# Attention and routed FFN on one core: inputs laid out by the host, attention weights expanded by VectorE and ScalarE in turn, softmax normalised earlier

## The reference, cut to what matters

```python
# x, ctx: (32, 128, 256) float32, 4096 tokens in 32 tiles of 128
# per token: 16 heads of 16 channels attend to each other inside the token
q = layernorm(x) @ Wq.T + bq ; k = ctx @ Wk.T + bk ; v = ctx @ Wv.T + bv
logits = einsum('bsid,bsjd->bsij', q, k) / 4        # 16 x 16 for every token
out = einsum('bsij,bsjd->bsid', softmax(logits), v)
x = x + transpose(out, (0, 2, 1, 3)).reshape(b, s, 256) @ Wd.T + bd
h = layernorm(x); gates = softmax((h @ w_red) @ normalised(wg).T)   # 8 experts
e = argmax(gates)                                    # one expert per token
x = x + (gelu(h @ W1[e] + b1[e]) @ W2[e] + b2[e]) * max(gates)
```

## Time and profile before

| | |
|---|---|
| median of 3 runs | 432.7 us |
| profiled execution | 430.04 us, span 428.1 us |
| PE, DVE, ACT, POOL busy | 89%, 73%, 55%, 69% of the span |
| granted TensorE clock, mean | 0.979 of full speed |
| DMA | 59.31 MB, 97433 packets |

### The profile page before, as it was taken

The page is one execution under the profiler, slowest core; times in us unless marked ns, Lnnn a source line. Parts: engine busy times, 40 slices in busy tenths (PEclk is TensorE's granted clock), DMA queues, the critical chain, the costliest instruction groups (busy, mean ns, idle before and its releaser), DMA issues.

```text
span 428.1 us, 11390 instructions
## 1 busy us (share of the span) xinstructions
PE 381.1 (89%) x3791; PEld 303.4 (71%) x3791; DVE 310.9 (73%) x667; ACT 234.8 (55%) x783; POOL 297.2 (69%) x399
## 2 busy tenths in 40 slices
PE   6996999999999989998888687978999999999980
PEld 6774676676766657565555466767999999999970
DVE  3746899899998989999999665579456555555640
ACT  4443778787686877776752564571344444444420
POOL 2767678787687877776775964656387777787751
PEclk9999999999999999999999899999899999999996
DMA  7696866978779787886566501131022222222200
GB/s 163 207 264 164 228 173 209 268 193 239 184 211 260 190 229 181 230 209 175 133 155 185 154 27 39 52 116 48 29 64 75 64 75 74 61 69 65 65 17 0
DMA packets 97433, 59.31 MB, mean 139 GB/s; under 512 B 70366, under 2 KB 88447, under 8 KB 97376
## 3 DMA queue, kind: packets, MB, share of 16 engines
q1 hardware_dynamic: 92368, 48.44, 41.8%
q0 software_dynamic: 3744, 9.53, 7.8%
q10 hardware_dynamic: 1264, 0.61, 0.8%
HBM read 37.41 MB, written 22.07 MB: 139 GB/s over the span
## 4 chain that ended last, share of the span: by engine, by line
PE 34%; DMA 24%; DVE 14%; issue 9%; SPq 9%; POOL 7%; ACT 2%; DVEq 1%; ACTq 0%; POOLq 0%
DMA qkv_scr<-qkv 21%; PE bQ L1107 14%; PE bKV L1075 8%; PE bL L1075 7%; SPq L248 4%; POOL kx L374 3%; SPq L252 2%; SPq L283 2%; DMA b2b<-in_L_ffn_wg 2%; DVE qkv L485 2%; PE bT L1089 2%; DVE qkv L492 1%; DMA ql<-qkv_scr 1%; PE bO L1057 1%; POOL r L420 1%
## 5 line engine op out<-in xcount | busy, mean ns | idle before, releaser
L374 POOL TENSOR_TENSOR kx<-ql,mask 128x2048 f32<-128x2048 f32 x32 | 117.6, 3675 | 42.7 <-issue 32.9
L1107 PE MATMUL bQ<-w,wA 128*128 x312 | 74.3, 381 | 3.4 <-DVE r L721 2.8
L475 DVE TENSOR_TENSOR ax<-bA,mask 128x2048 f32<-128x2048 f32 x32 | 73.3, 2290 | 0.6 <-PE bA L1013 0.6
L1107 PEld LDWEIGHTS bQ<-w,wA 128*128 128x128 f32 x312 | 56.2, 190 | 10.6 <-issue 4.5
L924 PE MATMUL bKV<-wA,xcT 128*128 128x512 f32 x128 | 60.2, 593 | 0.0
L397 POOL DMA_INDIRECT out<-r,isc x39 | 41.3, 1059 | 22.3 <-issue 13.4
L420 POOL DMA_INDIRECT r<-row_scr,ig x39 | 40.5, 1038 | 6.0 <-issue 2.4
L862 ACT ACTIVATE wA<-bL,r 128x128 f32<-128x128 f32 x76 | 21.6, 367 | 41.3 <-PE bL L1075 26.7
L862 ACT ACTIVATE wA<-bKV,r 128x128 f32<-128x128 f32 x80 | 22.8, 367 | 36.1 <-issue 18.8
L355 POOL TENSOR_TENSOR rs<-ve,half 128x2 f32<-128x2 f32 x39 | 28.3, 726 | 20.3 <-ACT ve L742 20.2
L932 PE MATMUL bL<-kx,pad 128*32 128x128 f32 x1024 | 35.8, 282 | 6.8 <-POOL kx L374 6.8
(11 more groups left out here) (202 smaller groups left out, 724.5 us busy)
## 6 DMA issues: line engine op xcount, KB each, us to landing
qkv_scr<-qkv SPq DMA_DIRECT2D x32, 384.0 KB, 4.2
ql<-qkv_scr SPq DMA_DIRECT2D x32, 384.0 KB, 4.6
row_scr<-cat SPq DMA_DIRECT2D x32, 133.5 KB, 3.6
w1b<-in_L_ffn_W SPq DMA_DIRECT2D x16, 256.0 KB, 4.5
w<-in_L_ffn_W SPq DMA_DIRECT2D x16, 256.0 KB, 4.7
xt<-in_x SPq DMA_DIRECT2D x15, 256.0 KB, 4.9
ct<-in_ctx SPq DMA_DIRECT2D x15, 256.0 KB, 4.9
b2b<-in_L_ffn_b SPq DMA_DIRECT2D x4, 256.0 KB, 4.7
```

The costliest lines, as they stand in the source:

```text
L374: eng.tensor_tensor(block(kx[:, z % 2, :]), spread_heads(ql[z % 2][:, :, 0:HD]), mask_b, ALU.mult).then_inc(S["kx"], 1)
L475: eng.tensor_tensor(block(ax[:, :]), spread_heads(bA[:, 0:C].rearrange("p (l i) -> p l i", l=NH)), mask_b, ALU.mult).then_inc(S["ax"], 1)
L1107: i_ = eng.matmul(bQ[:, 0:C], hT[b % 2][:, k, :], w2[:, bass.ds(eb * (KH * C) + k * C, C)], start=(k == 0), stop=(k == KH - 1))
```

## The change

The host passes other layouts of the same numbers: `xc` holds x and ctx turned (per pair of tiles, 4 KB in a row for each partition), `x` is given once more by rows, the weights `wkvT`, `wqT`, `wdT` are turned already, W1 and b1 come as one array and W2 with each partition's data in a row. The turning on TensorE and the copies to `xcT` go. The centring of Wq is made by a matmul with a constant matrix. x is thus read twice.

A ninth gate column (`NL = NE + 1`, each of its weights -1/256) gives minus the row mean out of the matmuls, so that `moments` of the new row needs no pass for the mean. The scaling by 1/256 and the epsilon move from ScalarE to GpSimd, whose two results go straight to `cat`.

`expand` on VectorE writes blocks 4 to 7 only; ScalarE writes blocks 0 to 3 in four instructions (`scalar_expand`) after it and behind `pad` and the row's scaling. This holds for the 28 tiles with `s1 + 4 < 32`; the last four stay on VectorE. Summing and scaling of the softmax (`normed`) stands behind the maximum and the expansion instead of at the end of the iteration; TensorE turns `a2` ahead of Wd. `fill` issues 16 in setup and 3 in each of iterations 0 to 3.

```diff
-EXT = C + NE
+NL = NE + 1
+EXT = C + NL
-CT = 6
+XC = 4
+SHARE = 4
...
         def sync_setup(eng):
-            for w, src in ((1, Wk), (2, Wv), (0, Wq)):
-                eng.dma_start(wst[w], src.rearrange("(a p) c -> p a c", p=P)).then_inc(S[f"ld_w{w}"], 16)
-            for k, src in enumerate((bk, bv, bq)):
-                eng.dma_start(bqkv[:, k, :], src.rearrange("(o n) -> o n", o=1).broadcast_to((P, C))
-                              ).then_inc(S["ld_b"], 16)
+            eng.dma_start(wT[:, :, 0:2 * C], wkvT).then_inc(S["ld_wkv"], 16)
+            eng.dma_start(wT[:, :, 2 * C:3 * C], wqT).then_inc(S["ld_wq"], 16)
+            eng.dma_start(bqkv[:, :, :].rearrange("p k c -> p (k c)"), bkvq.broadcast_to((P, 3 * C))
+                          ).then_inc(S["ld_b"], 16)
...
                 if live(n) and n % 2 == 0:
-                    eng.dma_start(xt[:, n % XR:n % XR + 2, 0:C], x[n:n + 2].rearrange("n p c -> p n c")
-                    eng.dma_start(ct[:, n % CT:n % CT + 2, :], ctx_in[n:n + 2].rearrange("n p c -> p n c")
+                    eng.dma_start(xt[:, n % XR:n % XR + 2, 0:C], x[n // 2]).then_inc(S[f"ld_x{n // 2 % 3}"], 16)
+                c = t + 3 if t > 0 else t + 5 if t == -3 else NT
+                if live(c) and c % 2 == 0:
+                    if c >= XC:
+                        eng.wait_ge(S["qq"], c - XC + 2)
+                    eng.dma_start(xcT[:, c % XC:c % XC + 2, :, :], xc[c // 2]).then_inc(S[f"ld_c{c // 2 % 2}"], 16)
...
+        def normed(eng, s0):
+            eng.wait_ge(S["exp"], s0 + 1)
+            eng.tensor_reduce(sm[:, :], pr.rearrange("p (g j) -> p g j", g=NH), AX, ALU.add).then_inc(S["sm"], 1)
...
...
+                if live(s1) and live(a):
+                    expand(eng, s1)
+                if live(s0) and live(a):
+                    normed(eng, s0)
                 if live(w):
                     eng.wait_ge(S["wd"], w + 1)
...
-                if live(s1) and live(a):
-                    expand(eng, s1)
                 if live(a) and t >= 4:
                     vector_kv(eng, a)
...
+        def scalar_expand(eng, s1):
+            eng.wait_ge(S["ax0"], s1 + 1)
+            for b in range(SHARE):
+                i_ = eng.activation(block(ax[:, :])[:, :, b, :], bA[:, 0:C].rearrange("p (l i) -> p l i", l=NH), ACT.Copy,
+                                    scale=mask[:, b:b + 1])
+            i_.then_inc(S["ax"], 1)
...
         def tensor_setup(eng):
             eng.wait_ge(S["ident"], 1)
-            fill(eng, 12)
-            weight_transposes(eng, 1)
-            tensor_turned(eng, 0)
-            fill(eng, 4)
-            weight_transposes(eng, 2)
-            fill(eng, 6)
-            weight_transposes(eng, 0)
+            fill(eng, 16)
...
                 if t < 4:
-                    fill(eng, 10, bA)
+                    fill(eng, 3, bA)
```

More of the change, by code:

```diff
@@ L73, in slotted, with build @@
     return 0 <= s < NS
-def build(nc, x, ctx_in, Wq, bq, Wk, bk, Wv, bv, Wd, bd, w_red, wg, W1, b1, W2, b2, out):
+def build(nc, x, xc, wkvT, wqT, wdT, Wd, bkvq, bd, bd_col, w_redT, wgT_in, wg, W1b, W2, b2, out):
     f32, bf16, i32 = mybir.dt.float32, mybir.dt.bfloat16, mybir.dt.int32
@@ L156, in build @@
         x0, x1 = fl(kx), fl(pad)
-        wst = [x0[:, 2048 + 512 * w:2560 + 512 * w].rearrange("p (a c) -> p a c", a=KC) for w in range(4)]
-        wrp, wrT = (b2b[:, k * C:(k + 1) * C].rearrange("p (a c) -> p a c", a=KC) for k in range(2))
+        wst = x0[:, 2048:2560].rearrange("p (a c) -> p a c", a=KC)
+        wrT = b2b[0:NG, 0:C]
+        mean = b2b[:, C:C + P]
         wrc = b2b[:, 4 * C:5 * C].rearrange("p (a c) -> p a c", a=KC)
@@ L298, in pool_setup @@
             eng.memset(ident[:, :], 0.0).then_inc(S["filled"], 1)
+            eng.memset(mean, -1.0 / C)
+            eng.memset(gate[:, :, NE:NL], -1.0 / C)
             eng.memset(half[:, :], -0.5)
@@ L480, in vector_kv @@
             if a == 0:
[L481 removed]
+                eng.wait_ge(S["ld_b"], 16)
             if a > 1:
@@ L1155, in _, with laid_out, blocks @@
                     tensor_inverse(eng)
-_INS = ["x", "ctx_1024", "L0_xattn_Wq", "L0_xattn_bq", "L0_xattn_Wk", "L0_xattn_bk", "L0_xattn_Wv",
-        "L0_xattn_bv", "L0_xattn_Wd", "L0_xattn_bd", "L0_ffn_w_red", "L0_ffn_wg", "L0_ffn_W1",
-        "L0_ffn_b1", "L0_ffn_W2", "L0_ffn_b2"]
+def laid_out(inputs, np):
+    def blocks(w, n):
+        return w.reshape(n, P, -1).transpose(1, 0, 2)
+    i = {k.replace("L0_xattn_", "").replace("L0_ffn_", ""): np.asarray(v) for k, v in inputs.items()}
+    x, ctx = i["x"], i["ctx_1024"]
+    xc = np.stack((x.reshape(NT, P, KC, P), ctx.reshape(NT, P, KC, P)), 2).transpose(0, 4, 2, 3, 1)
+    return {
+        "x": x.reshape(NT // 2, 2, P, C).transpose(0, 2, 1, 3),
+        "xc": xc.reshape(NT // 2, 2, P, 4, P).transpose(0, 2, 1, 3, 4),
+        "wkvT": np.concatenate((blocks(i["Wk"].T, KC), blocks(i["Wv"].T, KC)), 2),
+        "wqT": blocks(i["Wq"].T, KC),
+        "wdT": blocks(i["Wd"].T, KC),
+        "Wd": i["Wd"],
+        "bkvq": np.concatenate((i["bk"], i["bv"], i["bq"])).reshape(1, 3 * C),
+        "bd": i["bd"],
+        "bd_col": np.broadcast_to(i["bd"].reshape(KC, P).T[:, :, None], (P, KC, P)),
+        "w_redT": i["w_red"].T,
+        "wgT": i["wg"].T,
+        "wg": i["wg"],
+        "W1b": np.concatenate((i["W1"].reshape(NE, KC, P, HID).transpose(0, 2, 1, 3).reshape(NE, P, KC * HID),
+                               i["b1"].reshape(NE, KH, P).transpose(0, 2, 1)), 2),
+        "W2": i["W2"].reshape(NE, KH, P, C).transpose(0, 2, 1, 3).reshape(NE, P, KH * C),
+        "b2": i["b2"],
+    }
 def kernel(**inputs):
```

318 lines of the change are left out of this document (118 added, 200 removed).

## The result

The changed kernel is slower: 433.97 us (median of 20 runs) against 429.97 for the one before (20 runs). The ratio is 1.0072, with a 95% interval of 1.004 to 1.0104. All ratios in this document compare fast runs alone; here these have means of 433.17 and 430.08 us, and three slower runs of the changed kernel and one of 1331 us of the kernel before are left out. The forecast was 6.5 us faster, 426.2, with a range up to 433; measured is 3.1 us slower, so the sign was wrong too. (The 432.7 that the prediction started from was the median of three runs, and the 2.66 us that it added for the median's distance from the profiled execution are not there over 20 runs: 429.97 against 430.04.)

The account below looks back on a forecast made before the run. It took SyncE's store-and-load loop and a nearly equal three-iteration loop to bound tiles 4 to 23, VectorE the next tiles. Terms -3.8 + 2.0 - 4.2 - 0.5 = -6.5 us gave 426.2 us, range 417 to 433 (eight in ten).

Parts of the forecast that it names:

- What bounds the kernel: Tiles 4 to 23: SyncE's loop of 6.64 us without compute engines, beside a three-iteration loop of 6.66 us per iteration.
- the price of the loads in steady attention: Tiles 4 to 23: 256 KB more for two tiles cost 0.25 us, 0.12 per tile, bounds 0 and 0.25.
- The term for tiles 4 to 23: Steady attention: mean interval from 6.685 to 6.79 us, +2.0 us in all, ends -2 and +6.
- The prediction's own sign of being wrong: A first store after 15 us, steady intervals under 6.5 or over 7.1, or four expansions taking over 2 us.
- the ring-order sentence: Each DMA engine consumes descriptors in ring order; so loads issued behind a store cannot delay it, price nothing in SyncE's loop.
- The loads rival: Tiles 4 to 23: x read twice makes ql land later every second iteration, period 7.0, total 431.4 us; chance 0.17.
- The way through the engines: Three-iteration loop: 0.25 us added from ql to the maximum, 0.15 from the maximum to qad; 20.0 becomes 20.5.
- The slow rival: ScalarE's expansion waits behind pad and holds bO, bL and the maximum: period 7.23, total 438.8 us; chance 0.11.
- The engines rival: Engines were the true limit; freed, they let all intervals fall to about 6.45 us, total 417.4; chance 0.17.
- Tiles 23 to 31: VectorE, the bound, loses 1.1 us; interval falls from 7.58 to 7.05, -4.2 us, VectorE busy below 6.3.
- Setup: Start: wg issued sooner lands near 7 us, first store near 12 instead of 15.84, -3.8 us, range -5 to -1.
- Rest: Last tiles and first slots: ScalarE has 0.9 us less a tile, -0.5 us, range -2 to +1.5.

Follow-up runs that it names:

- loads_behind: Changed kernel with the loads of x and xc issued behind the load back of ql instead of ahead of it; ratio 1.0445 to the kernel before.
- expert_ahead: spread_xc with the half expert issued ahead of SyncE's wait for its store instead of behind the load back; ratio 0.9687 to the kernel before.
- after_no_x: Changed kernel without the loads of x by rows from tile 12 on, so its numbers are other ones; ratio 0.9802 to the kernel before.
- before_extra: Kernel before with one more 256 KB load of x, read by nobody, in each odd iteration from the third on; ratio 1.011 to the kernel before.
- before_ahead: Kernel before with only the half expert's issue moved ahead of SyncE's wait for its store; ratio 0.9862 to the kernel before.
- spread_share_off: spread_xc with the whole expansion on VectorE for all tiles and none on ScalarE; ratio 0.9975 to the kernel before.
- spread_norm_late: spread_xc with sum, inverse and scaling of the softmax back at the end of VectorE's iteration; ratio 0.9972 to the kernel before.
- odd_two: Changed kernel with the 512 KB load of xc as two DMAs of 256 KB in the same odd iteration; ratio 1.0151 to the kernel before.
- after_ahead: Changed kernel with only the half expert's issue moved ahead of SyncE's wait for its store; ratio 0.9773 to the kernel before.
- spread_both: spread_xc with x by rows also loaded one tile (128 KB) in every iteration; ratio 0.9898 to the kernel before.
- spread_xc: Changed kernel with xc loaded one tile (256 KB) in every iteration instead of two tiles in every second one; ratio 0.9876 to the kernel before.
- spread_wg_first: spread_xc with the gate's three small loads first on ScalarE's queue, ahead of xc and x of tile 0; ratio 0.992 to the kernel before.
- spread_setup: spread_xc with tile 0's xc first on SyncE's queue, the gate's loads first on ScalarE's, and 28 unused transposes instead of 16; ratio 0.9933 to the kernel before.

## Why the prediction was wrong

**What bounds the kernel.** Right: SyncE's loop of store, load back and expert, with no engine in it. The half expert's 1.25 us was taken for a cost of issuing. Most of it was a wait behind `ql`, as loads_behind and expert_ahead show (0.4 to 0.6 us once it stands elsewhere, but for a few of 1.1 to 1.3).

**The step that failed** is the price of the loads in steady attention: "512 KB cost about 0.5 us in a pair, and 256 KB more in larger pieces 0.25, or 0.12 per tile". It measured 0.81 us a pair (after against after_no_x), which is 0.40 per tile and above the upper end of 0.25; in the kernel before it was 0.45 a pair (before_extra). The term for tiles 4 to 23, +2.0 us with the ends -2 and +6, was +8.8, outside its own bounds. Of that 7.0 us came from tile 7 on, where after_no_x takes all of it back. The other 1.8 came in tiles 4 to 6 (21.3 us against 19.4), where after_no_x is no faster (21.9); no run takes that part apart. The fault was the linear step from one price to the next. Most of the idle fifth of the DMA engines lay in the even iterations (share 0.68, against 0.91 in odd ones), while the added bytes went into the odd ones. The share of a stretch says nothing on its halves. The prediction's own sign of being wrong, steady intervals over 7.1, came true.

Beside it stood the ring-order sentence from the Trainium skill (DMA: Bandwidth & Descriptors, "Queues, rings and completion order"). The conclusion that I drew from it, that loads behind the store cannot delay it, did not hold: the wait for the store grew from 4.70 to 5.17 in odd iterations, and fell to 4.21 in loads_behind. More of the loss, 0.76 us, came from the issue behind `ql`. What the rule says of order fits loads_behind, where the wait of the next store grew to 6.13 us with more ahead of it.

**The loads rival** named the mechanism and gave 431.4 with a period of 7.0. The period measured 7.15, and its price too was too small: it still had the whole 1.3 us faster, where 3.1 us slower was measured.

**The way through the engines.** I added 0.25 us from `ql` to the maximum and 0.15 from the maximum to `qad`. Neither came. On the mean of tiles 6 to 19 the first way (from `kx`) went from 4.97 to 4.88 us, the second from 5.32 to 5.17. The rows of tile 20 answer to the earlier trace rows and show why `kx` still covers ScalarE (GpSimd, ScalarE, TensorE; start us, us):

```profile
164.82 3.67 POOL L360 TENSOR_TENSOR kx<-ql,mask 128x2048 f32<-128x2048 f32 x1 [1.44 <-issue]
```
```profile
164.77 0.63 ACT L758 ACTIVATE pad<-ql 128x512 f32<-128x512 f32 x1 [0.57 <-DMA ql<-qkv_scr]
165.31 0.28 ACT L795 ACTIVATE cat<-cat 128x1 f32<-128x1 f32 x1
...
165.78 1.54 ACT L807 ACTIVATE ax<-bA,mask 128x256 f32<-128x256 f32 x4
```
```profile
167.37 1.08 PE L869 MATMUL bO<-ax,pad 128*32 128x128 f32 x32 [0.66 <-ACT ax L807]
168.55 1.08 PE L869 MATMUL bL<-kx,pad 128*32 128x128 f32 x32
```

`pad` and the row scaling overlap to 1.0 us instead of my 1.38, so `bO` starts 2.6 us behind `pad` and is done as `kx` ends at 168.49. The slow rival, the expansion holding everything, is thereby refuted; the period that it named, over 7.13, was reached by another cause. The expansion's four instructions took 1.54 us together, near the 1.46 I took.

**The engines rival** (engines were the true limit) is refuted: VectorE's work in tiles 4 to 23 fell by a fifth and the stretch grew. But once the expert's issue is out of the loop SyncE waits for q, as before_ahead and expert_ahead show.

**Tiles 23 to 31.** Right: 7.15 against 7.05 forecast. spread_share_off shows that the gain needs the shared expansion, spread_norm_late that it needs the early softmax too. VectorE is busy 6.46 us of an interval, not below 6.3.

**Setup.** Mis-sized: the first store gained 1.1 us, not 3.8, and the 1.1 holds for this trace alone. after_no_x, odd_two, loads_behind and after_ahead have the same setup and first stores at 16.01, 15.56, 15.60 and 14.78. In after_no_x the granted clock was 0.72 from 10.2 to 14 us, and the matmuls of q of tile 0 took 2.13 us instead of 1.16.

I also gave the shorter `fill` no price. From the first store to that of tile 4 the granted clock was 0.98 before and 0.86 after; from 38 to 44 us it stood at 0.50, the lower of its two levels, behind 4.25 us in which TensorE waited, and 32 matmuls of `bO` took 1.93 us instead of 1.08. In the same stretch it was 0.95 to 1.00 in the three kernels with 10 transposes in each early iteration and 0.83 to 0.92 in the thirteen with 3. No run changes that number alone, so what it costs is open.

What held the first store of the changed kernel shows in VectorE's rows. It waited until 9.88 for the last of three small loads on ScalarE's queue, the 0.5 KB of `wgT`, 7.0 us from its issue:

```profile
2.82 0.44 ACTq L731 DMA_DIRECT2D wgT<-in_wgT  x1
...
9.88 0.29 DVE L422 TENSOR_TENSOR b2b<-b2b 128x128 f32<-128x128 f32 x1 [6.25 <-DMA wgT<-in_wgT]
```

I had priced `wg` and overlooked that the new wait is for all three. **Rest** and **experts**: right within 1 us together, and the slots kept their 3.73 us.

**Left open.** 256 KB cost 0.45 us a pair in the kernel before and 0.81 in the changed one. odd_two excludes the DMA's size (14.18 a pair, against 14.40). The difference is about as large as the scatter of single traces, so it may be nothing. Nor is it known why spread_both is not below spread_xc. What in the DMA engines or queues makes `ql` and the store late behind more bytes was not looked into.

## What to carry to other kernels

Read the DMA share of a repeating pattern by its halves. Here 256 KB more in a half whose share was 0.92 without them (after_no_x) cost 0.81 us a pair, and moving half of xc into the half at 0.59 won 0.67 of it back. In a queue that waits for its own store, ask of each issue whether it stands between the wait and the next store; moving one such issue gave 1.4% to the kernel before and 2% to 3% to the changed one and spread_xc. When work is taken from engines, first see that the loop which sets the period has an engine in it.

## What the runs showed of the hardware that was not expected

- The first DMA issued behind the 2048-piece load `ql` occupies SyncE's queue for 1.2 to 1.7 us on the mean, or 2.1 to 2.4 when 768 KB were issued ahead of `ql`; the same issue mostly takes 0.4 to 0.6 us elsewhere.
- The first k/v matmuls took 3.64 us after a pause of 1.1 us behind 16 transposes, and 1.88 us behind 28. The profile's granted clock reads 1.00 of full speed in both stretches, so it doesn't show what differed. The time is what half the clock would give, as with `bO` at 0.50 above (1.93 against 1.08 us), but that is an inference.
- A 0.5 KB load took 7.0 us to land in setup, 5.4 when it was issued ahead of xc and x on its queue (spread_wg_first) and 4.0 when xc of tile 0 left that queue too (spread_setup).
